# One-expert tiles behind four mixed tiles, with high and low weight parts on the two partition halves

## What is computed

```python
x = x + jnp.tanh(g_xattn[0]) * _L0_xattn_ref(_layernorm(x), fside_BxS2xS2_0, ctx_1024)   # int8-style quantised MLP
x = x + jnp.tanh(g_ffn[0]) * _L0_ffn_ref(_layernorm(x), ...)

def _L0_ffn_ref(...):                       # H, I, E, K, R = 256, 896, 8, 2, 64; SCALING = 0.25
    bids = sigmoid(x @ conf_W.T + conf_b) * expert_wealth
    top_bids, sel = top_k(bids, K); routing = softmax(top_bids)
    base_g, base_u = x @ base_gate, x @ base_up
    for e in range(E):
        g = base_g + x @ gate_A[e] @ gate_B[e] * SCALING
        u = base_u + x @ up_A[e] @ up_B[e] * SCALING
        h = silu(g) * u
        oe = h @ base_down + h @ down_A[e] @ down_B[e] * SCALING
        out = out + we[..., None] * oe      # we: the token's share for expert e
```

## Time and profile before

| | us |
|---|---|
| median of 3 runs | 294.61 (293.88 to 296.35) |
| the profiled execution, whole | 293.96 |
| its span in the trace | 292.1 |
| TensorE busy in the span | 259.4 (89%) |
| VectorE busy | 199.8 (68%) |
| ScalarE busy | 160.7 (55%) |
| GpSimd busy | 132.1 (45%) |
| mean granted clock of TensorE | 0.967 of full |

### The profile page before, as it was taken

How to read it: one execution, slowest core, us unless ns; L and a number is a source line. 1 busy time by engine, 2 the same in 40 slices (tenths; PEclk the granted TensorE clock), 3 DMA queues, 4 the chain that set the end, 5 groups by cost and what they waited for, 6 DMA issues and landing times.

```text
span 292.1 us, 5362 instructions
## 1 busy us (share of the span) xinstructions
PE 259.4 (89%) x1625; PEld 237.9 (81%) x1626; DVE 199.8 (68%) x419; ACT 160.7 (55%) x291; POOL 132.1 (45%) x152
## 2 busy tenths in 40 slices
PE   0845676999999899899999999999999999999882
PEld 0745554889888789799999899999999999998882
DVE  2998789788157711966777566777666687766584
ACT  3346978987764344844455544455645445654440
POOL 4588548558754111314444728753333444230051
PEclk9998697799999999999999999999999999999998
DMA  6953423476989451744334361354444333440534
GB/s 172 315 155 86 127 74 87 128 226 223 298 268 330 161 194 69 266 144 137 95 133 144 103 238 44 138 177 153 152 144 162 108 107 145 144 144 18 176 132 144
DMA packets 31342, 45.69 MB, mean 156 GB/s; under 512 B 14104, under 2 KB 25760, under 8 KB 31328
## 3 DMA queue, kind: packets, MB, share of 16 engines
q0 software_dynamic: 4416, 21.50, 22.3%
q1 hardware_dynamic: 20752, 14.03, 17.6%
q10 hardware_dynamic: 6160, 9.98, 9.3%
HBM read 33.57 MB, written 11.93 MB: 156 GB/s over the span
## 4 chain that ended last, share of the span: by engine, by line
PE 63%; DVE 18%; DMA 6%; POOL 4%; ACT 4%; issue 3%; SPq 0%; DVEq 0%; ACTq 0%
PE pY L55 8%; PE pY L59 8%; PE pY L57 8%; PE pT L1627 5%; PE pG L55 3%; PE pU L57 3%; PE pU L59 3%; PE pG L59 3%; PE pG L57 3%; PE pU L55 3%; PE bank L55 2%; DMA x_resid<-in_x_dram 2%; PE bank L57 2%; PE bank L59 2%; DVE x_resid L1305 2%
## 5 line engine op out<-in xcount | busy, mean ns | idle before, releaser
L528 POOL DMA_INDIRECT results<-yb,dest x17 | 16.8, 991 | 71.6 <-DVE yb L1248 71.6
L55 PE MATMUL pY<-Wd_hi,hT_hi 128*128 128x384 f32 x126 | 45.1, 358 | 0.2
L59 PE MATMUL pY<-Wd_hi,hT_lo 128*128 128x384 f32 x126 | 42.3, 336 | 0.0
L57 PE MATMUL pY<-Wd_lo,hT_hi 128*128 128x384 f32 x126 | 42.3, 335 | 0.0
L783 ACT CAST xaT_hi<-pX 128x256 fp32r<-128x256 f32 x19 | 7.1, 373 | 47.1 <-PE pX L1602 47.1
L514 POOL DMA_INDIRECT xin<-normed,tok x19 | 18.8, 991 | 23.4 <-PE pX L1588 10.1
L522 POOL DMA_INDIRECT bin<-base_products,tok x18 | 21.1, 1170 | 16.6 <-issue 7.1
L807 ACT CAST hT_hi<-pT 128x896 fp32r<-128x896 f32 x19 | 17.2, 908 | 18.6 <-PE pT L1627 18.6
L55 PEld LDWEIGHTS pY<-Wd_hi,hT_hi 128*128 128x128 f32 x126 | 23.6, 188 | 1.4 <-issue 0.8
L55 PE MATMUL bank<-Wbase_hi,x2T_hi 128*128 128x448 f32 x64 | 24.5, 383 | 0.2 <-ACT brow L676 0.2
L676 ACT COPY brow<-bank 128x448 f32<-128x448 f32 x32 | 16.9, 531 | 13.0 <-PE bank L59 12.3
(11 more groups left out here) (284 smaller groups left out, 763.4 us busy)
## 6 DMA issues: line engine op xcount, KB each, us to landing
base_products<-brow ACTq DMA_DIRECT2D x16, 448.0 KB, 3.5
yr<-results SPq DMA_DIRECT2D x8, 256.0 KB, 4.6
raw<-in_L_ffn_gate_B_dram SPq DMA_DIRECT2D x8, 224.0 KB, 2.6
raw<-in_L_ffn_up_B_dram SPq DMA_DIRECT2D x8, 224.0 KB, 3.2
raw<-in_L_ffn_down_A_dram SPq DMA_DIRECT2D x7, 256.0 KB, 4.8
x_resid<-in_x_dram SPq DMA_DIRECT2D x4, 256.0 KB, 5.1
q<-in_fside_BxS2xS_dram ACTq DMA_DIRECT2D x4, 256.0 KB, 6.6
normed<-q ACTq DMA_DIRECT2D x4, 256.0 KB, 4.0
```

The source lines that it names most:

```text
L55: m.matmul(outs[i], hi, whi[i], start=first, stop=False, skip_group_check=True)
L57: m.matmul(outs[i], hi, wlo[i], start=False, stop=False, skip_group_check=True)
L59: ins = m.matmul(outs[i], lo, whi[i], start=False, stop=last, skip_group_check=True)
```

## The change

Sorting is by expert. Each group still has one tile in which its two experts are mixed, and these are now tiles 0 to 3. All other tiles, 4 to 18, hold pairs of one expert (`eid` in place of `gid`). `is_mixed(j)` tells them apart when the program is built.

In a one-expert tile the inner side of the second products is only 64 rows. The 64 rows of the input are put on the partitions twice, and the weights have their high part on one half of the partitions and their low part on the other, in one tensor (`WB`, `WdB`, with an index by expert). A product with the high input then gives high x (high + low), a second gives the low input's share: two products, not three. Project_A has 128 columns, not 256, and down_products H + R = 320.

The mixed tiles need both experts' rows on the 128 partitions, high and low in separate slots 2g and 2g+1. So weights are loaded in that layout, and SyncE turns it over while the mixed tiles run: for each pair it copies the high part's lower half and the low part's upper half to `turn_B` on the other partitions (`lower_out`), waits for that, waits until the mixed tile's expanding products are done, and copies them back crosswise (`crossed_in`). `turn_B` holds one pair, so the pairs go one after the other. `turn_dB` is the same for down_B, in one go.

The tile loop has another order on all engines. x_T of the next tile stands behind the first gate half; h_T is cut in two (four and three chunks) and belongs to the iteration of the next tile; the second gate half comes last of the four, ahead of the down products. ScalarE takes over both masks (now scales) and the copy of y; z is transposed into a free part of the bank of `pY`. On GpSimd gather(2) goes ahead of gather_base(1), and a scatter comes one tile later.

The core of the diff:

```diff
+        WB = sb("WB", [P, 2, E, I], F32R, wb_scope)
+            turn_B = sb("turn_B", [P, 2, I], F32, bin_scope)
+            turn_dB = sb("turn_dB", [P, G, H], F32, bin_scope)
...
+        def is_mixed(j):
+            return isinstance(j, int) and j < G
+        def down_cols(j):
+            return H + (GR if is_mixed(j) else R)
+        def z_bank(j):
+            return pX[:, 0:P] if isinstance(j, int) and j == PT - 1 else pY[:, H + GR:H + GR + P]
...
         @block.sync
+            def lower_out(to, w):
+                sp.dma_start(to[0:R], w(0)[R:P]).then_inc(d_lower, 16)
+                sp.dma_start(to[R:P], w(1)[0:R]).then_inc(d_lower, 16)
+            def crossed_in(w, held):
+                sp.dma_start(w(0)[R:P], held[R:P]).then_inc(d_turned, 16)
+                sp.dma_start(w(1)[0:R], held[0:R]).then_inc(d_turned, 16)
+            def pair_B(g):
+                return lambda a: WB[:, :, GE * g + a, :].bitcast(F32)
+            def pair_dB(a):
+                return WdB[:, a:E:GE, :].bitcast(F32)
+            sp.wait_ge(s_wlo, CH_1)
+            sp.wait_ge(s_direct, 1)
+            lower_out(turn_dB, pair_dB)
+            for g in range(G):
+                if g:
+                    sp.wait_ge(d_turned, 32 * g)
+                lower_out(turn_B, pair_B(g))
+                sp.wait_ge(d_lower, 32 * (g + 2))
+                sp.wait_ge(s_g, g + 1)
+                sp.wait_ge(s_u, g + 1)
+                crossed_in(pair_B(g), turn_B)
+            sp.wait_ge(d_turned, 32 * G)
+            sp.wait_ge(s_y, G)
+            crossed_in(pair_dB, turn_dB)
             sp.wait_ge(s_u, PT)
...
         @block.scalar
+            def xa_out(j):
+                act.wait_ge(s_A, j + 1)
+                if not (isinstance(j, int) and j == 0):
+                    act.wait_ge(s_xaT, j)
+                if is_mixed(j):
+                    for e in range(GE):
+                        ins = a.activation(xa[:, :, e, :], pX[:, H:2 * H].rearrange("p (a e r) -> p a e r", a=2, e=GE)[:, :, e, :],
+                                           ACT.Copy, scale=mask[:, j, e:e + 1])
+                else:
+                    ins = a.activation(xa[:, :, :, :], pX[:, H:H + P].rearrange("p (a r) -> p a r", a=2).unsqueeze(2).to_broadcast([P, 2, GE, R]),
+                                       ACT.Copy, scale=SCALING)
+                ins.then_inc(s_xac, 1)
...
             def tile(j, back2=True, back3=True, last=False):
-                g = group(j - 1)
-                h_hi(j - 1, not back2)
+                e = expert(j - 1)
+                down_A_expert(j - 1, 0, e)
                 if back2:
                     z_hi(j - 2, not back3)
-                down_A_group(j - 1, 0, g)
-                down_A_group(j - 1, 1, g)
                 if not last:
                     x_hi(j + 1)
+                h_hi(j - 1, 0, not back2)
+                down_A_expert(j - 1, 1, e)
+                if back2:
+                    y_out(j - 2, not back3)
+                h_hi(j - 1, 1)
+                if not last:
+                    xa_out(j + 1)
                 silu(j)
                 if not last:
                     xa_hi(j + 1)
+                z_out(j - 1, not back2)
...
         @block.tensor
+                    if isinstance(j, int) and j == G:
+                        pe.wait_ge(d_turned, 32 * G)
+                to, cols = (pG, pU)[gu][:, i, 0:IH], slice(i * IH, (i + 1) * IH)
+                x_hi, x_lo = xaT_hi[:, gu, :], xaT_lo[:, gu, :]
+                if is_mixed(j):
+                    ins = split_product([to], x_hi, x_lo, [WB[:, gu, e, cols]], [WB[:, gu, e + 1, cols]], not first, True)
+                else:
+                    wsl = WB[:, gu, at(e), cols].rearrange("p a w -> p (a w)")
+                    m.matmul(to, x_hi, wsl, start=True, stop=False, skip_group_check=True)
+                    ins = m.matmul(to, x_lo, wsl, start=False, stop=True, skip_group_check=True)
...
-            def h_T(j, first=False):
-                pe.wait_ge(s_h, j + 1)
+            def h_T(j, i, first=False):
+                if i == 0:
+                    pe.wait_ge(s_h, j + 1)
```

382 lines of the change are left out of this document (210 added, 172 removed).

## The result

| | us |
|---|---|
| before, median of 4 runs | 295.02 (293.88 to 296.35) |
| after, median of 4 runs | 320.33 (318.33 to 323.58) |
| ratio after to before | 1.083, 95% interval 1.074 to 1.093 |
| profiled execution after, whole | 319.1 |

What follows compares the result with a forecast made beforehand. TensorE was taken to set the time in the routed part. 293.96 - 22.5 + 1.5 - 0.5 - 0.7 gave 271.8, plus 3.9 wait for the turn and 1.7 clock: 277.4, said as 278 us; range 272 to 298.

Steps and rivals of the forecast that it cites:

- Expanding products, down products, second down step: TensorE products in one-expert tiles: four fewer, 320 columns for 384, two for three; savings of 12.2, 8.5 and 1.8 us.
- A one-expert tile takes 7.1 us: Tile loop on TensorE: 8.63 us less 0.81, 0.61 and 0.12 should give a period of 7.1 us.
- What hides the rest: One-expert tiles: VectorE and ScalarE at about 5 us each stay under 7.1; the 4.3 us chain is covered, 0.6 spare.
- Routing, +1.5 us and a wait of 2.2: Counting per expert on VectorE adds 1.5 us (0 to 4.8); TensorE waits 2.2 instead of 0.74 us before sorting products.
- Without anything new, 271.8 us: Whole kernel without the cost of the turn: 293.96 - 22.5 + 1.5 - 0.5 - 0.7 = 271.8 us.
- a step with its wait is 1.25 + 2.3 + 0.1 = 3.65: SyncE's turn of the weights: 1.25 us fixed, 2.3 data per pair; first step 4.95, seven more 25.5 us.
- the rival of half the rate: Turn transfers on 64 partitions reach half the ways: step 5.95 us, wait 20 to 24, time 293 to 297; chance 0.30.
- Four gathers of base rows: Gathers beside the turn add 1 us each, moving its end from 146.4 to 150.4; TensorE waits 3.9 us at tile 4.
- The sign: Whole kernel against before: faster by more than 1% at chance 0.64, within 1% at 0.16, slower at 0.20.
- The turn starts at 115.9: SyncE begins the turn when tile 0's base products are done, 114.35, plus 1.5 us of routing.
- Clock, 1.7 us: TensorE after the wait ahead of tile 4: a low stretch at 1.2 GHz, partly in the wait, costs 1.7 us.
- the turn at half rate with the gathers in full: Rival: half rate plus 2.3 us per gather and 0.5 per step; turn ends 179.3, wait 33, time 306; chance 0.10.

Runs made afterwards that it cites:

- the interleaved turn: The changed kernel with a pair's two experts on even and odd partitions, so each turn transfer takes every second partition: 303.68 us, 1.028 of before.
- the bench: Copies between bin and turn_B timed alone behind the output of the kernel without the turn: two on 64 neighbours 6.18 us, two on 128 3.93 us.
- the way by DRAM: The changed kernel with half transfers out to a DRAM scratch tensor behind the last weights, four steps back: 295.64 us, 0.9985 of before.

## Why the prediction was wrong

By its own steps, in their order:

- *Expanding products, down products, second down step.* Right: distances of 0.203, 0.146 and 0.12 us. The line through the three widths held at 320 columns.
- *First projection, taken as nothing.* Right: products of 128 columns start 0.11 us apart, those of 256 before 0.118.
- *A one-expert tile takes 7.1 us.* 7.43 to 7.47 was measured. The 0.3 us are the load of the expert index right ahead of the projection; with the load moved it is 7.11. I hadn't priced this instruction at all, and in 14 tiles it is 4.5 us.
- *What hides the rest.* Right: in the loop no wait on VectorE or ScalarE opens.
- *Routing, +1.5 us and a wait of 2.2.* Right. The wait was 2.18 us. From counting to tile 0 pass 21.87 us instead of 19.0; without the low clock behind the wait (kernel without a turn) 20.28, so +1.3, and the low clock is the other 1.6.
- *Without anything new, 271.8 us.* The kernel without its turn was profiled at 276.38. The index loads, 4.5 us, are as large as this difference. Its four executions took 276.38 to 281.64, so the agreement within 0.1 us is partly luck.
- *The turn: "A pair is 0.917 MB, 2.3 us of data; a step with its wait is 1.25 + 2.3 + 0.1 = 3.65."* This step failed. On 64 neighbouring partitions it is 6.2 us, since the rate is 195 and not 402 GB/s. On 128 the figure would have held (3.9). I had given this 0.30 as the rival of half the rate, with a step of 5.95, but taken the full rate because no row of before showed a 64-partition transfer slow; neither did any show one fast.
- *"Four gathers of base rows (0.917 MB each) run beside it; I add 1 us for each."* This step failed too. Beside a full-rate turn the gathers of a tile cost 4 us (7.6 to 8.1 for 3.9), so that even the interleaved turn waits 18.7 us and gives 303.7. I had priced them by the 400 GB/s of the best slices of the earlier trace rows; but the row of issues in the same group has 5.5 us to landing, and 1.16 MB hold the engines for 4.3 us.
- *The sign.* Either of the two is enough for it. With the full rate and the gathers 303.7 us was measured. With the half rate and no time for the gathers the turn would end at 119.9 + 52 = 172, and the wait would be 17.4 us in place of 29.9: some 307, which is an estimate from the steps of the bench.
- *The turn starts at 115.9.* It was 119.9: about 2 us later in the first stage, whose code is unchanged (the product on q2T starts 2.1 us later, and between 61.0 and 64.6 in the other kernels), and most of the rest in the routing with its low clock. Nothing in the change explains the first.
- *Clock, 1.7 us.* 2.6 behind the stall. Two more stretches weren't forecast: 1.6 behind the routing wait, and 1.7 behind the wait for the low part of h (granted clock 0.59, 0.50, 0.50 and 0.71 of full in the four us from 135).

The sum of the turn, by what the runs showed: eight steps at 6.2 and 2.7 for the WdB transfers in the first are 52 us; measured were 64.5 (119.9 to 184.4), so 12.5 belong to the gathers and scatters beside it. My sum had 30.5 and 4. In the profiled execution 319.1 - 277.4 = 41.7 us are missing. Tile 4 starts at 184.5 instead of 150.4, 34.1 us later: 4.0 by the later start of the turn and 30.1 by its length. What held TensorE up while the turn ran, the 2.1 us for the low part of h in tile 1, whose base rows landed late, and the low stretch behind it, only shortened the wait ahead of tile 4. Behind it come 4.5 us in the loads of the index, 2.3 in a wait for tokens (at 204.78) and 0.9 more at the low clock than forecast. That makes 41.8.

Of the rivals, "the turn at half rate with the gathers in full" (179.3, 33 us, 306) was the one that came, at 0.10. Its mechanism was right, and its turn of 63.4 us is close to the 64.5 measured. Its end is 5 us early, 4 of them by the start of the turn, and its wait 3 us too long, since TensorE came to tile 4 at 154.6 and not at 146.5. Its time is 13 us low: these 5, and the 7.7 behind the stall (index loads, tokens, clock), which no path of the prediction had.

## What to carry to other kernels

Lay out rows that DMA must move so that each transfer spans all 128 partitions; 64 rows on every second partition are as fast as 128, while 64 neighbours run at half the rate. Price a new transfer by the time that the DMA engines have left in that stretch, not by its bytes at the best rate: what counts for indirect transfers is their share of the engines' time (here 3.4 to 4.3 us a tile). Rounds through one buffer with a wait each turn every such delay into a serial one; issue the outward half early, where the engines are idle, and in portions that a latency-bound gather can pass. This last advice isn't shown piece by piece: the way by DRAM changed the buffer, the number of rounds and the start of the way out together, and only the portions were tested alone.
